# PixArt block, six of eight input batches read with features first and normalised by GpSimd, tail splits two banks at a time

## The reference

```python
# x [8, 512, 512], ctx [8, 512, 512], cond [8, 512]; _layernorm over the last axis, eps 1e-5
def _mingru(x, Wz, bz, Wh, bh):
    z = jax.nn.sigmoid(jnp.einsum('bsi,hi->bsh', x, Wz) + bz)
    h_tilde = jnp.tanh(jnp.einsum('bsi,hi->bsh', x, Wh) + bh)
    a = jnp.clip(1.0 - z, CLAMP_LO, CLAMP_HI)
    return _linear_scan(a, z * h_tilde)          # h_t = a_t h_(t-1) + b_t along the sequence

def _stack(x, Wz, bz, Wh, bh, gamma, beta):
    h = x
    for i in range(L):                            # L = 4 layers
        h_new = _mingru(h, Wz[i], bz[i], Wh[i], bh[i])
        if i > 0:
            h_new = h_new + h
        h = _layernorm(h_new, gamma, beta)
    return h

# called with Wz = Wh = ctx and bz = bh = cond, the same for both directions
h_fwd = _stack(x, ...)
h_bwd = flip(_stack(flip(x), ...))
xcond = concat([h_fwd, h_bwd]) @ fusion_W.T + fusion_b
x = x + xcond(_layernorm(x))
x = x + ffn(_layernorm(x))     # 512 -> 2048, exact gelu, layernorm, 2048 -> 512, ternary weights
```

## Time and profile before

| | before |
|---|---|
| median of 3 runs | 1540.54 us (1540.24 to 1540.54) |
| the profiled execution | 1540.21 us |
| its span on the core | 1538.4 us |
| PE busy | 1518.7 us (99%) |
| DVE busy | 1307.8 us (85%) |
| ACT busy | 1021.6 us (66%) |
| POOL busy | 829.6 us (54%) |
| granted TensorE clock | full, 2.4 GHz, all the time |

### The profile page before, as it was taken

The page is one execution under the profiler, slowest core; times in us unless marked ns, Lnnn a source line. Parts: engine busy times, 40 slices in busy tenths (PEclk is TensorE's granted clock), DMA queues, the critical chain, the costliest instruction groups (busy, mean ns, idle before and its releaser), DMA issues.

```text
span 1538.4 us, 22933 instructions
## 1 busy us (share of the span) xinstructions
PE 1518.7 (99%) x7744; PEld 1202.7 (78%) x7744; DVE 1307.8 (85%) x2021; ACT 1021.6 (66%) x1688; POOL 829.6 (54%) x1013
## 2 busy tenths in 40 slices
PE   9999999999999999999999999999999999999999
PEld 7877888888888888888888877777777777777776
DVE  8998999999899989999888887786877777776786
ACT  7988789898687897787987444445454444444354
POOL 6766657578868678676788632331423333332331
...
DMA packets 73157, 113.20 MB, mean 74 GB/s; under 512 B 5193, under 2 KB 37961, under 8 KB 69970
## 3 DMA queue, kind: packets, MB, share of 16 engines
...
...
## 4 chain that ended last, share of the span: by engine, by line
PE 50%; DVE 2%; ACT 1%; issue 0%; POOL 0%; DVEq 0%; ACTq 0%; POOLq 0%
PE ps L639 15%; PE ps L620 14%; PE ps L572 11%; PE ps L499 6%; PE ps L519 1%; PE ps L585 1%; PE ps L533 1%; PE ps L649 1%; DVE bnp L1132 1%; PE ps L662 0%; ACT H L876 0%; DVE H L1120 0%; DVE yb L1112 0%; ACT AH L880 0%; DVE H L1121 0%
## 5 line engine op out<-in xcount | busy, mean ns | idle before, releaser
L499 PE MATMUL ps<-AH,WH 128*128 128x512 f32 x896 | 366.9, 409 | 7.8 <-DVE H L1121 6.1
L499 PE MATMUL ps<-AL,WH 128*128 128x512 f32 x896 | 351.0, 392 | 0.0
L499 PE MATMUL ps<-AH,WL 128*128 128x512 f32 x896 | 349.4, 390 | 0.0
L1587 POOL TENSOR_TENSOR H<-H,yb 128x512 f32<-128x512 f32 x192 | 245.9, 1291 | 8.5 <-DVE yb L1112 1.3
L1112 DVE TENSOR_TENSOR_SCAN yb<-ab,ps 128x512 f32<-128x512 f32 x192 | 231.9, 1208 | 15.5 <-POOL ab L1578 9.1
L950 ACT ACTIVATE g<-ps 128x512 f32<-128x512 f32 x128 | 76.5, 598 | 248.7 <-PE ps L620 248.7
L837 ACT ACTIVATE yb<-ps,ncnd 128x512 f32<-128x512 f32 x224 | 158.2, 706 | 87.3 <-PE ps L499 84.2
L499 PEld LDWEIGHTS ps<-AH,WH 128*128 128x128 f32 x896 | 168.5, 188 | 46.3 <-DVE H L1121 8.6
L1307 DVE SCALAR_TENSOR_TENSOR gl<-g,wbcol,gh 128x512 fp32r<-128x512 f32 x118 | 116.9, 991 | 97.7 <-ACT gh L960 97.6
L499 PEld LDWEIGHTS ps<-AL,WH 128*128 128x128 f32 x896 | 168.1, 188 | 37.1
L1688 POOL TENSOR_TENSOR rs<-mv,nhalf 128x1 f32<-128x1 f32 x32 | 43.0, 1342 | 282.2 <-DVE mv L1279 282.2
...
## 6 DMA issues: line engine op xcount, KB each, us to landing
hs_scratch<-H SPq DMA_DIRECT2D x16, 1024.0 KB, 5.4
...
xr<-in_x SPq DMA_DIRECT2D x32, 256.0 KB, 4.5
out<-ob SPq DMA_DIRECT2D x32, 256.0 KB, 2.2
xbuf<-in_x SPq DMA_DIRECT2D x7, 1024.0 KB, 7.6
RAW<-in_wt SPq DMA_DIRECT2D x16, 256.0 KB, 6.3
stg<-in_fct SPq DMA_DIRECT2D x16, 256.0 KB, 3.2
stg<-in_pjt SPq DMA_DIRECT2D x16, 256.0 KB, 2.9
```

Source lines behind the costliest of these rows:

```text
L499: r = e.matmul(GATE[i % 3][:], w[:, q, m * 128:(m + 1) * 128], a[:, q, :], start=(n == 0), stop=(n == 11))
L1587: e.tensor_tensor(H[s][:, m, :], H[s][:, m, :], yb[i % 5][:], ALU.add).then_inc(s_v, 1)
```

## The change

1. The input x is given a second time with features first (`xt`, transposed on the host). For batches 2 to 7 the rows of x are loaded for the statistics alone; then `load_turned` loads the 1 MB of `xt` into the same `xbuf`.
2. Mean and 1/sigma of each token go to a scratch in HBM (`put_moments`, two DMAs of 512 single elements) and come back as rows that all partitions hold (`xrow`, two DMAs of 256 KB, in `load_turned`).
3. POOL subtracts the mean row and multiplies with the 1/sigma row: `center_x` and `scale_x`, for each of four tiles 128x512, in place. ACT writes `AH` in two instructions 128x1024 (`high_x`), DVE `AL` in two (`low_x`). `norm_x`, `back("x", ...)`, and `feature` and `low` of x go for these batches.
4. The statistics come earlier: for an even batch in DVE's slot J - 5, for the odd one behind it in slot J - 3 of the even one. The rows of both share `xbuf`, so the turned load of an even batch waits until the statistics of the odd batch behind it are done.
5. For f tails, `feature_pair` writes H twice and then `AH` of two neighbouring PSUM banks in one instruction 128x1024, and `low_pair` writes `AL` of both in one. Where the pair starts at bank 7 the two are still written apart. The order of the blocks is 0, 1, 2, 3 in place of 2, 0, 1, 3.
6. In DVE's slot, `low(f, 2)` stood ahead of `scan(job(s - 2), 1)`; now the scan is first, and both pairs stand ahead of `stats(f, 0)`, where `low(f, 3)` stood behind it.

```diff
+def even(b):
+    return b is not None and b % 2 == 0
+def measured(s):
+    if even(batch(s + 5)):
+        return batch(s + 5)
+    return batch(s + 3) + 1 if even(batch(s + 3)) else None
...
-RING_SLOT = [("B", "x", -2, 2), ("B", "b", 3, 2), ("B", "f", 2, 2), ("B", "f", 2, 0), ("B", "f", 2, 1),
-    ("B", "x", -1, 0), ("B", "b", 3, 3), ("B", "f", 2, 3), ("B", "b", 3, 1), ("B", "x", -1, 1), ("B", "b", 3, 0),
-    ("T", "f", 1, 0), ("T", "b", 1, 0), ("T", "b", 2, 1), ("T", "f", 1, 1), ("B", "x", -2, 3)]
-NORM_SLOT = [("b", 4, 0), ("f", 4, 1), ("x", -1, 0), ("f", 3, 0), ("b", 4, 1)]
-FEAT_SLOT = [("b", 5, 2), ("x", 1, 0), ("f", 4, 2), ("f", 4, 0), ("f", 4, 1), ("x", 1, 3), ("b", 5, 3), ("f", 4, 3),
-    ("b", 5, 1), ("b", 5, 0), ("x", 1, 1), ("x", -1, 2)]
-LOW_SLOT = [("f", 4, 2), ("x", 0, 2), ("x", 1, 3), ("x", 1, 0), ("f", 4, 0), ("f", 4, 1), ("b", 5, 3), ("b", 5, 1),
-    ("f", 4, 3), ("x", 1, 1), ("b", 5, 0), ("b", 4, 2)]
+RING_SLOT = [("B", "b", 3, 2), ("B", "f", 2, 0), ("B", "f", 2, 1), ("B", "b", 3, 3), ("B", "f", 2, 2), ("B", "f", 2, 3),
+    ("B", "b", 3, 1), ("B", "b", 3, 0), ("T", "f", 1, 0), ("T", "b", 1, 0), ("T", "b", 2, 1), ("T", "f", 1, 1)]
...
-            back("x", batch(s + 2), 2)
             back("h", tail_b(s - 3), 2)
             mm(job(s), 1)
-            back("h", tail(s - 2), 2)
             back("h", tail(s - 2), 0)
             back("h", tail(s - 2), 1)
-            back("x", batch(s + 1), 0)
             back("h", tail_b(s - 3), 3)
+            back("h", tail(s - 2), 2)
             back("h", tail(s - 2), 3)
             mm(job(s), 2)
             back("h", tail_b(s - 3), 1)
-            back("x", batch(s + 1), 1)
             back("h", tail_b(s - 3), 0)
             tokens(tail(s - 1), 0)
             tokens(tail_b(s - 1), 0)
             mm(job(s), 3)
             tokens(tail_b(s - 2), 1)
             tokens(tail(s - 1), 1)
-            back("x", batch(s + 2), 3)
...
+        def high_x(b, h):
+            if b is None:
+                return
+            s, p = 2 * (b % 2), slice(2 * h, 2 * h + 2)
+            e.wait_ge(s_xk, 4 * (b - 2) + 2 * h + 2)
+            if h == 0:
+                e.wait_ge(s_mm, 4 * JOB[(b - 2, 0, 3)] + 4)
+            e.activation(AH[s][:, p, :], xbuf[:, p, :], ACT.Copy).then_inc(s_xh, 1)
+        def feature_pair(idx, p):
+            if idx is None or layer(("h", idx)) == 3:
+                return
+            n, s = BANK[("h", idx, 2 * p)], place(TAILS[idx])
+            for m in (2 * p, 2 * p + 1):
+                e.wait_ge(s_t2, T2N[("h", idx, m)] + 1)
+                e.activation(H[s][:, m, :], RING[BANK[("h", idx, m)] % 5][:], ACT.Identity, bias=bet[:, m:m + 1],
+                             scale=gam[:, m:m + 1]).then_inc(s_h, 1)
+            if RING_PS[n % 5] < 7:
+                e.activation(AH[s][:, 2 * p:2 * p + 2, :], two_banks(n), ACT.Copy).then_inc(s_ah, 2)
+                return
+            for m in (2 * p, 2 * p + 1):
+                e.activation(AH[s][:, m, :], RING[BANK[("h", idx, m)] % 5][:], ACT.Copy).then_inc(s_ah, 1)
...
-            feature("x", batch(s - 1), 0)
-            feature("h", tail(s - 4), 2)
-            feature("h", tail(s - 4), 0)
-            feature("h", tail(s - 4), 1)
-            feature("x", batch(s - 1), 3)
+            high_x(batch(s), 0)
+            feature_pair(tail(s - 4), 0)
             feature("h", tail_b(s - 5), 3)
-            feature("h", tail(s - 4), 3)
+            feature_pair(tail(s - 4), 1)
             feature("h", tail_b(s - 5), 1)
             feature("h", tail_b(s - 5), 0)
             gates(job(s - 2), 2)
             if s == 57:
                 whole(0)
-            feature("x", batch(s - 1), 1)
             sizes(s, 1)
             made(s)
-            norm_x(batch(s + 1))
             norm(tail(s - 3), 0)
             gates(job(s - 2), 3)
+            high_x(batch(s), 1)
             norm(tail_b(s - 4), 1)
-            feature("x", batch(s + 1), 2)
...
+        def low_x(b, h):
+            if b is None:
+                return
+            s, p = 2 * (b % 2), slice(2 * h, 2 * h + 2)
+            e.wait_ge(s_xh, 2 * (b - 2) + h + 1)
+            e.tensor_tensor(AL[s][:, p, :], xbuf[:, p, :], AH[s][:, p, :].bitcast(F32), ALU.subtract).then_inc(s_xl, 1)
+        def low_pair(idx, p):
+            if idx is None or layer(("h", idx)) == 3:
+                return
+            n, s, m = BANK[("h", idx, 2 * p)], place(TAILS[idx]), slice(2 * p, 2 * p + 2)
+            if RING_PS[n % 5] == 7:
+                low("h", idx, 2 * p)
+                low("h", idx, 2 * p + 1)
+                return
+            e.wait_ge(s_ah, HIGHS[("h", idx, 2 * p + 1)])
+            e.tensor_tensor(AL[s][:, m, :], two_banks(n), AH[s][:, m, :].bitcast(F32), ALU.subtract).then_inc(s_al, 2)
...
-            low("h", tail(s - 4), 2)
-            low("x", batch(s), 2)
-            low("x", batch(s - 1), 3)
+            low_x(batch(s - 1), 1)
             scan(job(s - 2), 1)
-            low("x", batch(s - 1), 0)
-            low("h", tail(s - 4), 0)
-            low("h", tail(s - 4), 1)
+            low_pair(tail(s - 4), 0)
             low("h", tail_b(s - 5), 3)
+            low_pair(tail(s - 4), 1)
             stats(tail(s - 3), 0)
             low("h", tail_b(s - 5), 1)
-            low("h", tail(s - 4), 3)
             stats(tail_b(s - 3), 0)
-            low("x", batch(s - 1), 1)
             low("h", tail_b(s - 5), 0)
             stats(tail_b(s - 4), 1)
             blend(job(s - 2), 2)
             stats(tail(s - 3), 1)
             scan(job(s - 2), 2)
-            input_stats(batch(s + 2))
+            input_stats(measured(s))
+            low_x(batch(s), 0)
...
+        def center_x(b, q):
+            if b is None:
+                return
+            if q == 0:
+                e.wait_ge(d_xt, 16 * (b - 1))
+                e.wait_ge(d_rm, 32 * (b - 1))
+            e.tensor_tensor(xbuf[:, q, :], xbuf[:, q, :], xrow[:, 0, :], ALU.subtract).then_inc(s_xc, 1)
+        def scale_x(b, q):
+            if b is None:
+                return
+            e.wait_ge(s_xc, 4 * (b - 2) + q + 1)
+            e.tensor_tensor(xbuf[:, q, :], xbuf[:, q, :], xrow[:, 1, :], ALU.mult).then_inc(s_xk, 1)
...
+            center_x(batch(s + 1), 1)
+            center_x(batch(s), 3)
+            inv_x(measured(s - 1))
             add(job(s - 3), 2)
+            scale_x(batch(s + 1), 1)
+            scale_x(batch(s), 3)
             add(job(s - 3), 3)
             keep(job(s - 2), 1)
             remains(s - 1)
             pieces(s - 1)
+            center_x(batch(s + 2), 0)
             add(job(s - 2), 0)
+            center_x(batch(s + 1), 2)
             inv(tail(s - 3), 0)
             if s == 58:
                 addx(0)
             keep(job(s - 2), 2)
+            scale_x(batch(s + 2), 0)
+            scale_x(batch(s + 1), 2)
...
+        def put_moments(b):
+            e.wait_ge(s_xr, b + 2)
+            e.dma_start(xrow_v[b, 0], mvx[:, b % 2, :, 0], allow_slow_non_contiguous=True).then_inc(d_xo, 16)
+            e.dma_start(xrow_v[b, 1], rs[:, b % 2, :], allow_slow_non_contiguous=True).then_inc(d_xo, 16)
+        def load_turned(b):
+            if b % 2 == 0:
+                e.wait_ge(s_xs, 4 * b + 8)
+            else:
+                e.wait_ge(s_xl, 2 * (b - 2))
+            e.dma_start(xbuf[:], xt_v[b]).then_inc(d_xt, 16)
+            e.wait_ge(d_xo, 32 * (b - 1))
+            if b == 2:
+                e.wait_ge(s_gp, 2)
+                e.wait_ge(s_fr, L - 1)
+            else:
+                e.wait_ge(s_xk, 4 * (b - 2))
+            for r in range(2):
+                e.dma_start(xrow[:, r, :], xrow_hbm[b, r].partition_broadcast(128)).then_inc(d_rm, 16)
...
+            if even(batch(s + 5)):
+                load_x(batch(s + 5) + 1)
+            if measured(s - 1) is not None:
+                put_moments(measured(s - 1))
+            if even(batch(s + 3)):
+                load_turned(batch(s + 3))
+            if even(batch(s - 1)):
+                load_turned(batch(s - 1) + 1)
```

52 lines of the change are left out of this document (38 added, 14 removed), and 4 rows, old and new, of the table START_RING.

## The result

| | before | after |
|---|---|---|
| median | 1540.54 us | 1609.03 us (1604.21 to 1609.20, 4 runs) |
| ratio | | 1.0437, 95% interval 1.0418 to 1.0457 |
| span of the profiled execution | 1538.4 us | 1607.3 us |
| PE idle in the span (span less busy) | 19.7 us | 74.2 us |
| mean granted clock | 1.000 | 0.992 |

What follows compares the result with a forecast made beforehand. PE was taken to bound the kernel. 1540.2 - 11.2 (transposes) + 35.0 (POOL and load) + 2 + 3.3 + 4.6 (new order) = 1573.9, less 4 for overlap: 1570 us, range 1541 to 1590.

Steps and rivals of the forecast that it cites:

- What leaves PE: On PE, 24 `back` of x go, 96 of 880 transposes, at 0.47 us per `back`: 11.2 us gained.
- ACT and DVE by themselves: On ACT and DVE, fewer instructions for x and pairs instead of singles: lighter, counted at nothing.
- What POOL gets: POOL gets eight tensor_tensor per batch, 60 us in all, in its fullest slots; with the load wait PE loses 35.0 us.
- R4: Rival: POOL's new tensor_tensor take 1.6 us each, 14 us more in its full slots: 1584 us; chance 0.1.
- The wait for the load: At `center_x` of batches 4 and 6, rows land 9.2 us after the load's issue; POOL waits some 7 and 4 us.
- R3: Rival: loads are in time, only POOL's own work delays; without 8.2 and 3.5 us in batches 4 and 6, 1558; chance 0.2.
- The new order: New order of the splits on DVE, in three terms: 2, 3.3 and 4.6 us lost.
- (a): Plain slots: the pair ends 0.1 us before PE needs the bank, no wait; later statistics cost 2 us (0 to 6).
- (b): Layer-0 slots, with two scans: the pair ends about 1 us after PE wants the bank; 3.3 us in all.
- (c): Slots behind a layer-0 job: `tokens` wait for a bank that the second pair frees later; 4.6 us in all.
- R1: Rival: the transposes' time arrives whole, 1529 us; chance 0.12.
- R2: Rival: POOL's work fits in, but the new order costs its 8 to 10 us: 1539, no change; chance 0.08.

Runs made afterwards that it cites:

- e17: e15's kernel also without the load of xt, `high_x` and `low_x`, so batches 2 to 7 have only PE's layer-0 matmuls as input work: 1531.0 us.
- e15: e12's kernel without the statistics of batches 2 to 7, their `inv_x`, x load, moment stores and row loads: 1544.5 us.
- e12: Changed kernel with the former order of splits and without POOL's 48 instructions (`center_x`, `scale_x`); loads and moment stores stay: 1549.4 us.
- e3: Changed kernel with the former order of blocks and splits (single banks, first `low` ahead of the scan); the turned input stays whole: 1580.8 us.
- e16: e12's kernel with 96 unread identity transposes given back to PE in the two slots before a layer-0 job: 1550.7 us.
- e6: e3's kernel with the load of xt for batches 4 and 6 ahead of `load_raw` in SP's queue: 1575.0 us.
- e19: Changed kernel with only the load of xt for batches 4 and 6 moved ahead of `load_raw` in SP's queue: 1603.1 us.
- e2: Kernel before with only the new order of blocks and splits and the pairs on ACT and DVE, nothing added on POOL: 1574.5 us.
- e11: Kernel before with a tail's last `low` (block 3) ahead of its statistics on DVE, which come 0.67 us later: 1550.5 us.

## Why the prediction was wrong, step by step

Medians in a row, from the kernel before to the changed one, beside the terms of my sum:

| step | measured | forecast |
|---|---|---|
| transposes and all input work gone (e17) | -9.5 | -11.2 |
| xt's load, `high_x`, `low_x` (e15 - e17) | +13.5 | 0 |
| statistics, moments, rows (e12 - e15) | +4.9 | 0 |
| POOL's 48 and the wait for the load (e3 - e12) | +31.4 | +35.0 |
| new order and pairs (after - e3) | +28.2 | +9.9, less 4 overlap |
| sum | +68.5 | +29.7 |

The order in which parts are taken off matters by some us: the last row is 20 without POOL's work, and 34 in the kernel before. The stretches of lower clock are inside the rows: 0, 3.4, 0, 5.1 and 3.4 us of them, by the traces.

**What leaves PE: right.** The rate of 0.47 us per `back` gives 11.2, and 9.5 arrived where nothing took it. In e12, without POOL's work and in the former order, it is worth 1.3 us (e16), since PE then waits for DVE; in the changed kernel itself it was not tried.

**"ACT and DVE by themselves", which I counted "at nothing": the first failed step, 18 us.** I compared the number of instructions and their busy time, and not where they stand; the statistics' new places, the stores and the rows had no term at all. Each `low_x` takes DVE at once what two `low` took in two places, and both stand ahead of the scans of the layer-0 job. There DVE sets PE's pace: PE's largest wait in the kernel before is the one for that scan, and I read it only as small. The waits for it grew from 6.0 to 10.4 us between e17 and e15; that `low_x` is what makes them grow is argued from its place, since e15 has its load and `high_x` as well. It also takes longer than the 1.20 us that I took; see the last section.

**What POOL gets: right in size, in part by luck.** The late loads, 11.7 us of my term, gave back 6 when mended, so that about 25 of the 31.4 are POOL's own work, where I had 23.3, and 5.1 of the 31.4 are clock. In all 31.4 us against 35.0, in batches 2 and 3 together 8.1 (forecast 6.0), 4 and 5 13.4 (17.4), 6 and 7 10.3 (11.6), by the delays of e3 less those of e12. The durations were right as well:

```profile
L1720 POOL TENSOR_TENSOR xbuf<-xbuf,xrow 128x512 f32<-128x512 f32 x24 | 30.9, 1290 | 1.0
L1713 POOL TENSOR_TENSOR xbuf<-xbuf,xrow 128x512 f32<-128x512 f32 x24 | 30.8, 1284 | 11.2 <-DMA xrow<-xrow_scratch 10.2
```

1.29 us each, so rival R4 (1.6 us) falls. My words for POOL were "without idle time through slots J - 1 and J". For J = 27, POOL's busy time in PE's slots 25, 26 and 27 (fifth engine) is 12.20 of 14.10, 12.22 of 12.90 and 11.11 of 17.00 us: nearly true of the second, and of the others not, where POOL idles 1.9 and 5.9 us.

```profile
423.30:437.40 14.10, 12.97 (x68) 10.63 (x66) 10.25 (x17) 6.61 (x12) 12.20 (x13) 1.00 0.03 9
437.40:450.30 12.90, 12.90 (x67) 10.56 (x65) 12.25 (x19) 5.94 (x10) 12.22 (x13) 1.00 0.34 127
450.30:467.30 17.00, 14.88 (x83) 12.24 (x81) 14.81 (x22) 12.78 (x21) 11.11 (x19) 1.00 0.41 148
```

**The wait for the load: right for batch 4, wrong for batch 6.** On POOL, and SP's issues of the load and the rows:

```profile
392.43 1.26 POOL L1733 TENSOR_TENSOR stg<-raw,stg 128x512 f32<-128x512 f32 x1
399.99 1.29 POOL L1713 TENSOR_TENSOR xbuf<-xbuf,xrow 128x512 f32<-128x512 f32 x1 [6.30 <-DMA xrow<-xrow_scratch]
...
391.20 0.33 SPq L1979 DMA_DIRECT2D raw<-in_fct  x1
391.58 0.43 SPq L1933 DMA_DIRECT2D xbuf<-in_xt  x1
392.12 0.92 SPq L1941 DMA_DIRECT2D xrow<-xrow_scratch  x2
```

The load does stand behind `load_raw(9)`, the rows are there 8.3 us after its issue (I took 9.2; my 369.5 and 9.2 make 378.7, not 378.9, which changes nothing), and POOL waits 6.3 us (forecast "some 7"). At batch 6 it waits 0.2 us and not 4: the rows came 6.9 us after the load's issue, and POOL itself was later by then. A wait of 3.7 us at batch 2 I had not forecast. Taken out (e6, e19), the late loads give back 6 us, where my sum gives R3's 12. The even batches do add more delay than the odd ones in the table above (9.3, 19.4 and 12.6 us against 6.3, 8.3 and 7.5), but their stretches are nine slots or more against five, and only at batch 4 is POOL's wait for the load a large one.

**The new order: the second failed step, 22 us.** In (a) I worked through one plain slot, 37, in which the pair ends 0.1 us before PE needs it, and wrote "no wait" for all plain slots. Many slots have no such 0.1 us, and e2's trace has 17 waits for the pair, 22.7 us in all:

```profile
PE ps L525 <- DVE AL L1175: 22.7, 17, 2.4
PE ps L505 <- DVE H L1140: 4.0, 6, 0.7
```

15.8 of the 22.7 stand in plain slots, where I had none: 7.3 in the five slots in which DVE has statistics of an input ahead (15, 24, 29, 38, 43), 5.0 in slots 21, 35 and 49, and 3.5 in slots 5 and 7. In slots 21, 35 and 49 DVE itself waits 1.58 us for ACT's copy of two banks, as here in slot 35:

```profile
572.70 1.23 DVE L1175 TENSOR_TENSOR AL<-ps,AH 128x1024 fp32r<-128x1024 f32 x1 [1.58 <-ACT AH L898]
```

Terms (b) and (c) were right in size: the layer-0 slots have 4.7 us of waits for `low` in e2, single ones included (forecast 3.3), the slots behind them 3.5 (forecast 4.6). The failed one is (a).

For the statistics behind the pairs I wrote 2 us (0 to 6); less than half of that shift costs 10.0 (e11). My range could not hold it: its upper end left the order at its forecast, and added only the bounds of the load and R4's price.

**The clock: a term that was missing,** 12 us in after, inside the rows of the table as said there.

Rivals R1 and R2 fell: PE's idle time rose by 54.5 us, and its waits for `low` alone by 34, where R2 has them rise by the 11 us of the transposes. R3 fell at batch 4, where `center_x` waits for a DMA.

**What stays open.** Between e17 and e15, 4.4 of the 13.5 us are PE's longer wait for the second scan (10.4 against 6.0), and 3.4 the clock; the two of e15's ten executions that had the full clock throughout took 1540.5 us, 4 us under its median. How the rest divides between `low_x`, `high_x` and the load was not tried one by one. Nor was the store of 4-byte elements apart from the statistics; both with the rows are 4.9 us.
